# Tridiagonal reduction on one core: the next column as K times a packed vector less a part formed behind the inner product

## The reference

```python
deg = jnp.sum(A, axis=0) + jnp.sum(A, axis=1) - jnp.diagonal(A)
d_inv_sqrt = jnp.where(deg > 0, jax.lax.rsqrt(deg), 0.0)
L_norm = d_inv_sqrt[:, None] * (jnp.diag(deg) - A) * d_inv_sqrt[None, :]
_, U = jnp.linalg.eigh(L_norm)          # A is 128x128
agg = jnp.einsum('mn,bnd->bmd', U.T, features)
h = jax.nn.relu(agg @ W1 + b1)
out = jnp.einsum('nm,bmd->bnd', U, h @ W2 + b2)
```

## Time and profile before

| what | value |
|---|---|
| median of three runs | 1530.33 us (1529.59 to 1530.63) |
| profiled execution, its own time | 1528.6 us |
| its span | 1526.9 us |
| VectorE busy | 1127.4 us, 74% of the span |
| TensorE busy | 1196.6 us, 78% |
| ScalarE busy | 796.6 us, 52% |
| GpSimd busy | 511.0 us, 33% |

### The profile page before, as it was taken

The page is one execution under the profiler, slowest core; times in us unless marked ns, Lnnn a source line. Parts: engine busy times, 40 slices in busy tenths (PEclk is TensorE's granted clock), DMA queues, the critical chain, the costliest instruction groups (busy, mean ns, idle before and its releaser), DMA issues.

```text
span 1526.9 us, 26214 instructions
## 1 busy us (share of the span) xinstructions
PE 1196.6 (78%) x7121; PEld 1070.4 (70%) x7121; DVE 1127.4 (74%) x6077; ACT 796.6 (52%) x2572; POOL 511.0 (33%) x1426
## 2 busy tenths in 40 slices
PE   5666777777616600069999999999999999999998
PEld 4555666666515500058889899898998989989897
DVE  8999999999999999977757655555465555645545
ACT  1222222222319900002478687786877868778676
POOL 0288888888888888830000200000000000000000
PEclk9999999999959955569999999999999999999999
DMA  9300000000000000003100000000000000000001
GB/s 268 77 1 0 1 1 1 1 1 1 1 0 2 1 0 1 0 14 97 56 1 1 28 0 14 14 0 28 0 14 14 0 27 0 14 13 0 28 1 29
DMA packets 43625, 28.76 MB, mean 19 GB/s; under 512 B 1520, under 2 KB 39440, under 8 KB 43536
## 3 DMA queue, kind: packets, MB, share of 16 engines
q1 hardware_dynamic: 43536, 27.81, 6.7%
HBM read 19.42 MB, written 8.39 MB: 18 GB/s over the span
## 4 chain that ended last, share of the span: by engine, by line
PE 57%; DVE 38%; issue 3%; ACT 2%; ACTq 0%; DVEq 0%
PE bank L794 13%; PE bank L784 10%; PE bank L789 8%; PE bank L797 7%; PE bank L601 6%; DVE PV L1192 5%; DVE RC L1186 4%; DVE PV L1122 2%; DVE wB L935 2%; PE bank L714 2%; PE bank L766 2%; PE bank L758 2%; PE bank L722 2%; DVE sc L945 2%; PE bank L729 2%
## 5 line engine op out<-in xcount | busy, mean ns | idle before, releaser
L794 PE MATMUL bank<-spare,wT 128*128 128x256 f32 (+2 forms) x1408 | 311.2, 321 | 0.0
L530 ACT ACTIVATE PV<-bank,bias 128x256 f32<-128x256 f32 (+2 forms) x704 | 304.9, 436 | 0.0
L530 ACT ACTIVATE BIG<-bank,bias 128x128 f32<-128x128 f32 (+2 forms) x544 | 228.2, 419 | 120.2 <-PE bank L797 101.2
L794 PEld LDWEIGHTS bank<-spare,wT 128*128 128x128 f32 x1408 | 234.8, 191 | 13.2
L784 PE MATMUL bank<-spare,wT 128*128 128x128 f32 (+2 forms) x1088 | 228.1, 320 | 4.1 <-DVE spare L1429 2.7
L1415 DVE TENSOR_TENSOR BIG<-BIG,PV 128x128 f32<-128x128 f32 (+2 forms) x192 | 63.0, 328 | 206.0 <-ACT BIG L530 205.9
L784 PEld LDWEIGHTS bank<-spare,wT 128*128 128x128 f32 x1088 | 168.7, 190 | 22.5 <-DVE spare L1429 9.1
L797 PE MATMUL bank<-spare,wT 128*128 128x128 f32 (+2 forms) x768 | 169.7, 303 | 0.0
L424 ACT ACTIVATE sc<-bank 128x1 f32<-128x1 f32 x127 | 21.7, 171 | 262.3 <-PE bank L596 262.3
L596 PE MATMUL bank<-ident 128*128 128x2 f32 x254 | 74.4, 363 | 92.8 <-DVE ident L951 91.6
L789 PE MATMUL bank<-spare,wT 128*128 128x128 f32 (+2 forms) x768 | 141.6, 307 | 3.7 <-DVE spare L1427 1.2
(11 more groups left out here) (393 smaller groups left out, 2756.7 us busy)
## 6 DMA issues: line engine op xcount, KB each, us to landing
spare<-in_x SPq DMA_DIRECT2D x32, 256.0 KB, 4.1
out<-X SPq DMA_DIRECT2D x32, 256.0 KB, 2.4
spare<-in_L_gnn_Wih SPq DMA_DIRECT2D x4, 256.0 KB, 5.1
spare<-in_L_gnn_Whh SPq DMA_DIRECT2D x4, 256.0 KB, 5.0
W<-in_L_gnn_W SPq DMA_DIRECT2D x2, 64.0 KB, 2.5
Wg<-in_L_gnn_Wg SPq DMA_DIRECT2D x2, 64.0 KB, 2.2
adj<-in_adj SPq DMA_DIRECT2D x1, 64.0 KB, 1.8
X<-in_x SPq DMA_DIRECT2D x4, 0.5 KB, 17.1
```

Source lines behind the costliest of these rows:

```text
L530: last = nc.scalar.activation(gate_out[q][i][:, 0:T], gate(i, q, T), ACT.Tanh if q == GATE_G else ACT.Sigmoid, bias=bias[:, at:at + 1])
L794: last = nc.tensor.matmul(gate(i, q, T), wT[:, 0, p - 1, q * D:(q + 1) * D], xt, start=True, stop=(j == 0))
```

## The change

Three columns are no longer scaled as one triple. `UC` column 0 now holds the mask itself (not its negative). Two packed pairs are formed: (`HUM`, `HU`) = (x below the pivot, u) times h, and (`HV`, `HG`) = (mask, x below the pivot) times u_t times h, the latter as a tensor_scalar whose two scalars are both read from memory, one value per partition. Behind the inner product stand `PT` = (Au)_t HUM - ACOL, `R` = p HV + PT, `NHP` as before, and x = HG K - R. `V1`, `Z` and `T2` are gone. The wait for ScalarE's row copy moves from the inner product to the first pair. The column `ACOL` is now made by ScalarE, as an activation Copy with the mask as its scale, between L425 and L428, behind a wait for the update of `A`; VectorE waits for it ahead of the inner product. ScalarE's wait for `e_ready` goes, and the small operands count on the semaphore of the weights.

```diff
--- before.py
+++ after.py
@@ -125,7 +125,6 @@
         x_in = [sem(f"x_in{c}") for c in range(X_CHUNKS)]
         tables = sem("tables")
         weights_in = sem("weights_in")
-        small_in = sem("small_in")
         w_turned = sem("w_turned")
         w_kept = sem("w_kept")
         small_turned = sem("small_turned")
@@ -171,6 +170,7 @@
         u_ready = sem("u_ready")
         p_ready = sem("p_ready")
         a_ready = sem("a_ready")
+        acol_ready = sem("acol_ready")
         leaf_ready = sem("leaf_ready")
         leaf_sign = sem("leaf_sign")
         to_pe = sem("to_pe")
@@ -188,8 +188,8 @@
         block = ctx.enter_context(nc.Block())
 
         STEPS = N - 1
-        ST, DEN, SGE1, SGE, K3, NHP, V1, T2, Z, ACOL = range(10, 20)
-        HB, HUM, HU = range(20, 23)
+        ST, DEN, SGE1, SGE, K3, NHP, PT, R, ACOL = range(10, 19)
+        HUM, HU, HV, HG = range(20, 24)
 
         def two_sigma(k):
             return sc[:, 24 + k % 2:25 + k % 2]
@@ -273,12 +276,12 @@
...
-                sp.dma_start(t[:], t_in[name]).then_inc(small_in, 16)
+                sp.dma_start(t[:], t_in[name]).then_inc(weights_in, 16)
...
@@ -418,11 +421,11 @@
             nc.scalar.activation(m[5][:], m[4][:], ACT.Sqrt).then_inc(rs_out, 1)
             for k in range(STEPS):
                 t = k + 1
-                if k >= 2:
-                    act.wait_ge(e_ready, k - 1)
                 act.wait_ge(s_ready, k + 1)
                 nc.scalar.activation(two_sigma(k), banks[7][:, 1:2], ACT.Sqrt, scale=4.0).then_inc(sigma_ready, 1)
                 nc.scalar.activation(half_x(k), banks[7][:, 0:1], ACT.Abs, scale=0.5).then_inc(sigma_ready, 1)
+                act.wait_ge(a_ready, k + 1)
+                nc.scalar.activation(S_(ACOL), A[:, t:t + 1], ACT.Copy, scale=below[:, t:t + 1]).then_inc(acol_ready, 1)
                 if t + 1 < N:
                     act.wait_ge(xb_ready, k + 1)
                     nc.scalar.activation(uB[:, k % 2, t + 1:N], banks[0][:, t + 1:N], ACT.Copy).then_inc(row_ready, 1)
@@ -633,7 +636,7 @@
             nc.tensor.matmul(B[4], QU, QV, start=True, stop=False)
             nc.tensor.matmul(B[4], ident[:, 0:N], ident[:, 0:N], start=False, stop=True).then_inc(q_pe, 1)
 
-            pe.wait_ge(weights_in, 16 * 2 * SKIPS)
+            pe.wait_ge(weights_in, 16 * (2 * SKIPS + 10))
             for c in range(2 * SKIPS):
                 if c >= 2:
                     pe.wait_ge(w_kept, c - 1)
@@ -641,7 +644,6 @@
                     last = nc.tensor.transpose(banks[c % 2][:, q * D:(q + 1) * D], w_nat[:, c // SKIPS, c % SKIPS, q, :],
                                                ident[:, 0:N])
                 last.then_inc(w_turned, 1)
-            pe.wait_ge(small_in, 16 * 10)
             pe.wait_ge(w_kept, 2 * SKIPS)
             nc.tensor.transpose(banks[0][:, 0:N], adj[:], ident[:, 0:N])
             K = 4 * SKIPS
@@ -880,7 +882,7 @@
             V.tensor_copy(sc[:, 40:41], sc[:, 1:2]).then_inc(x_ready, 1)
 
 
-            op(V.tensor_scalar(UC[:, 0:N - 1, 0], below[:, 1:N], -1.0, None, ALU.mult))
+            op(V.tensor_copy(UC[:, 0:N - 1, 0], below[:, 1:N]))
             h = Tally(hv)
 
             def step(ins):
@@ -908,8 +910,6 @@
 
                 if k >= BN_LAG:
                     x_statistics(k - BN_LAG)
-                dve.wait_ge(a_ready, k + 1)
-                step(V.tensor_tensor(S(ACOL), A[:, nxt], below[:, nxt], ALU.mult))
                 dve.wait_ge(sigma_ready, 2 * k + 1)
                 dve.wait_ge(hv, before)
                 V.scalar_tensor_tensor(out=u_c, in0=S(SGE), scalar=sigma2, in1=x_c,
@@ -919,44 +919,42 @@
                 n_st = step(V.tensor_scalar(S(ST), s, TINY, None, ALU.add))
                 V.tensor_scalar(sg, x_t, 0.0, 0.5, ALU.is_ge, ALU.subtract).then_inc(sg_ready, 1)
                 dve.wait_ge(hv, n_st)
-                n_neg = step(V.scalar_tensor_tensor(out=S(DEN), in0=half_x(k), scalar=sigma2, in1=S(ST),
+                n_den = step(V.scalar_tensor_tensor(out=S(DEN), in0=half_x(k), scalar=sigma2, in1=S(ST),
                                                     op0=ALU.mult, op1=ALU.add))
                 dve.wait_ge(sg_ready, k + 1)
                 n_ut = step(V.scalar_tensor_tensor(out=u_t, in0=sg, scalar=sigma2, in1=x_t, op0=ALU.mult, op1=ALU.add))
-                dve.wait_ge(hv, n_neg)
+                dve.wait_ge(hv, n_den)
                 n_h = step(V.reciprocal(h_k, S(DEN)))
                 dve.wait_ge(hv, n_h)
                 dve.wait_ge(u_ready, k + 1)
-                n_nh = step(V.tensor_tensor(S(HB, 3), UC[:, k, :], h_k.to_broadcast([N, 3]), ALU.mult))
-
-                dve.wait_ge(pb_ready, k + 1)
                 if t + 1 < N:
                     dve.wait_ge(row_ready, k + 1)
-                n_k = step(V.tensor_tensor_reduce(out=wB[:, live(k)], in0=banks[1][:, live(k)], in1=uk[:, live(k)],
-                                                  scale=h_k, scalar=0.0, op0=ALU.mult, op1=ALU.add,
-                                                  accum_out=S(K3)))
-                dve.wait_ge(hv, n_nh)
-                n_v = step(V.tensor_tensor(S(V1), S(HB), u_t, ALU.mult))
-                dve.wait_ge(hv, n_k)
-                n_z = step(V.scalar_tensor_tensor(out=S(Z), in0=u_t, scalar=S(K3), in1=B[1][:, nxt],
-                                                  op0=ALU.mult, op1=ALU.subtract))
+                n_hu = step(V.tensor_tensor(S(HUM, 2), UC[:, k, 1:3], h_k.to_broadcast([N, 2]), ALU.mult))
+                n_hv = step(V.tensor_scalar(S(HV, 2), UC[:, k, 0:2], u_t, h_k, ALU.mult, ALU.mult))
+
+                dve.wait_ge(pb_ready, k + 1)
+                dve.wait_ge(acol_ready, k + 1)
+                step(V.tensor_tensor_reduce(out=wB[:, live(k)], in0=banks[1][:, live(k)], in1=uk[:, live(k)],
+                                            scale=h_k, scalar=0.0, op0=ALU.mult, op1=ALU.add, accum_out=S(K3)))
+                dve.wait_ge(hv, n_hu)
+                n_pt = step(V.scalar_tensor_tensor(out=S(PT), in0=B[1][:, nxt], scalar=S(HUM), in1=S(ACOL),
+                                                   op0=ALU.mult, op1=ALU.subtract))
+                dve.wait_ge(hv, n_pt)
                 dve.wait_ge(p_ready, k + 1)
-                dve.wait_ge(hv, n_v)
-                n_t2 = step(V.scalar_tensor_tensor(out=S(T2), in0=banks[2][:, 0:1], scalar=S(V1), in1=S(ACOL),
-                                                   op0=ALU.mult, op1=ALU.add))
+                n_r = step(V.scalar_tensor_tensor(out=S(R), in0=banks[2][:, 0:1], scalar=S(HV), in1=S(PT),
+                                                  op0=ALU.mult, op1=ALU.add))
                 n_nhp = step(V.scalar_tensor_tensor(out=S(NHP), in0=banks[2][:, 0:1], scalar=-1.0, in1=h_k,
-                                            op0=ALU.mult, op1=ALU.mult))
-                dve.wait_ge(hv, n_t2)
-
-                V.scalar_tensor_tensor(out=x_c, in0=S(HUM), scalar=S(Z), in1=S(T2),
-                                       op0=ALU.mult, op1=ALU.add).then_inc(x_ready, 1)
+                                                    op0=ALU.mult, op1=ALU.mult))
+                dve.wait_ge(hv, n_r)
+                V.scalar_tensor_tensor(out=x_c, in0=S(HG), scalar=S(K3), in1=S(R),
+                                       op0=ALU.mult, op1=ALU.subtract).then_inc(x_ready, 1)
                 dve.wait_ge(hv, n_nhp)
-                step(V.scalar_tensor_tensor(out=A[:, live(k)], in0=uk[:, live(k)], scalar=S(NHP), in1=A[:, live(k)],
+                n_a = step(V.scalar_tensor_tensor(out=A[:, live(k)], in0=uk[:, live(k)], scalar=S(NHP), in1=A[:, live(k)],
                                                   op0=ALU.mult, op1=ALU.add))
                 n_wb = step(V.scalar_tensor_tensor(out=wB[:, live(k)], in0=uk[:, live(k)], scalar=S(K3),
                                                    in1=banks[1][:, live(k)], op0=ALU.mult, op1=ALU.subtract))
                 n_sge1 = prepare_sign(k + 1) if k + 1 < STEPS else None
-                dve.wait_ge(hv, n_wb)
+                dve.wait_ge(hv, max(n_a, n_wb))
                 V.scalar_tensor_tensor(out=A[:, live(k)], in0=wB[:, live(k)], scalar=S(HU), in1=A[:, live(k)],
                                        op0=ALU.mult, op1=ALU.add).then_inc(a_ready, 1)
                 return prepare_row(k + 1, n_sge1) if k + 1 < STEPS else None
```

More of the change, by code:

```diff
@@ L204, in live, with S_ @@
             return slice(k + 1, N)
+        def S_(i):
+            return sc[:, i:i + 1]
         d16, e16 = leaf[:, 0:16], leaf[:, 16:32]
@@ L275, in _ @@
             for t, name in ((W1, "L0_gnn_W1"), (W2, "L0_gnn_W2"), (Wg0, "L1_gnn_Wg0"), (Wg1, "L1_gnn_Wg1")):
-                sp.dma_start(t[:], t_in[name]).then_inc(small_in, 16)
+                sp.dma_start(t[:], t_in[name]).then_inc(weights_in, 16)
             for t, name in ((b2B, "L0_gnn_b2"), (bg0B, "L1_gnn_bg0"), (bg1B, "L1_gnn_bg1")):
```

(6 more changed lines are left out.)

## The result

The changed kernel takes 1526.91 us (median, 1525.73 to 1527.49) against 1530.12 us for the kernel before on the same chips: ratio 0.9979, 95% interval 0.9971 to 0.9986. It is 3.2 us faster, clear of zero by the interval; 2.4 us slower, within what can be told from no change, was forecast. Its profiled execution took 1526.4 us with a span of 1524.7 us.

A forecast was written before the change was run, and what follows sets the result against it. One dependent loop through three engines, 127 steps of 2.99 us, was taken to bound the kernel. Pairs +6.1 less ACOL off VectorE 3.7 gave +2.4 us: 1532.7 against the median 1530.33, range 1527.5 to 1537.5.

The forecast's parts named there:

- ACOL on ScalarE: ScalarE's column copy, covered by TensorE's product, the dropped `e_ready` wait and the joined load semaphore: zero for all.
- Two pairs: Ahead of the inner product: first to second place needs 0.26 us, has 0.12 to 0.27; 6.1 us lost.
- ACOL off VectorE: Ahead of u (L915): the copy's slot leaves VectorE's queue; 3.7 us gained, bounds 2.6 to 7.6.
- The 1.1 us of the early steps: In 16 early steps L915 waits only for L974, 0.19 us behind it instead of 0.26; 1.1 us gained.
- Behind the inner product: Accumulator's read to new column: 0.50 us against 0.51; nothing gained or lost, bounds plus or minus 2.5 us.
- The rivals: Alternatives to the first case (chance 0.60): cheaper two-scalar slot, operation count, engine held to its end, PT held by the read.
- not 0.14 or 0.06: Second pair's two-scalar slot costs no more than one scalar, or nothing: 1528.7 or 1526.6 us; chance 0.15.
- the engine isn't held to its end: Rival: the inner product can't start before the two-scalar operation ends, place needs 0.35; 1542.7 us, chance 0.15.
- `PT` starts at the same stamp as the accumulator's read: Rival behind the inner product: PT is held by the accumulator's read, 0.08 a step, 10.2 us; 1542.9, chance 0.05.
- one VectorE operation fewer is a gain: Rival: operation count decides, 7 one-column operations between root and new x instead of 8; 7.6 us, 1522.7, chance 0.05.
- What the profile after would show: Signs: u 0.19 behind the mask's operation early; inner product 0.26 behind the first pair; late steps 0.09 to 0.14 longer.

The follow-up runs named there:

- r2: Changed kernel with ScalarE's wait for `e_ready` put back ahead of the wait for `s_ready`: 1531.39 us, ratio 1.0011 to the kernel before.
- r6: Kernel before with only the two pairs and PT, R in place of the triple and V1, Z, T2: ratio 1.0026 to the kernel before.
- r5: Changed kernel with the column copy ACOL back on VectorE, ahead of u: ratio 1.0009 to the kernel before.
- r4: Changed kernel with the two waits ahead of u (L915) swapped, VectorE's own counter first, the root second: ratio 1.0007 to the kernel before.
- r12: Changed kernel with the first pair's waits reordered: u_ready, VectorE's own counter, then row_ready: ratio 1.0022 to the kernel before.
- r11: Changed kernel with TensorE's two waits ahead of the product swapped, update of A first, u second: ratio 1.0002 to the kernel before.
- r3: Changed kernel with the wait for `e_ready` put back, but behind the wait for `s_ready`: 1527.06 us, ratio 0.9982 to the kernel before.

## Why the prediction was wrong

The step that failed is in "ACOL on ScalarE": the dropped wait for `e_ready` "asked for something two steps old", so its removal was priced at zero. That the condition had long been true was right. That the wait was therefore free was not: written first, it pushed the wait for `s_ready` into an instruction of its own, 0.06 us a step. With that wait put back in its place (r2) the kernel after loses all its gain; its removal is worth 4.9 us by time (4.4 in the loop). Added to the forecast's +2.4, it gives -2.5, near the -3.2 measured.

Added up along one path of ratios, with 1530 us as the whole (each ratio's interval is about 1.5 us to either side, so a difference of two has about 2): pairs alone +4.0 us (r6), then `ACOL` to ScalarE and the joined load semaphore -2.3 (to r2; no run has the semaphore alone), then the wait for `e_ready` away -4.9 (to the kernel after), -3.2 together.

- **Two pairs**: mechanism right, +6.1 forecast, +4.0 measured (+4.8 in the loop) for the whole of r6. The place needs 0.27 to 0.29, near the forecast 0.26. Ahead of the inner product the loss was forecast too small, not too large: +7.8 us, with 3.9 instead of 3.7 up to width 32 and 3.4 instead of 2.4 at widths 33 to 86. The slot of the two-scalar operation, put at 0.20 from two durations in the earlier trace rows, measured 0.19.
- **ACOL off VectorE**: -3.7 forecast, -2.3 measured with the wait for `e_ready` in place (-2.8 in the loop), -4.2 in the loop without it (r5 to after). A part counts for more once the other is gone, since u starts at the later of the two: the queue and the root. The 1.1 us of the early steps didn't come, since L915's second written wait took the slot over; with the other order they did (r4: 46.7 us instead of 47.8).
- **Behind the inner product**: zero forecast, -2.5 us in r6 and -2.4 in the kernel after, at the end of the stated bounds. At width 32 it is 0.50 us against 0.51, but 40 of 127 steps of the kernel before lie above 0.51 and only 4 of the kernel after. Why those steps are longer stays open. The two errors, ahead of the inner product and behind it, offset each other, so it is in part luck that the sum for the pairs came so near.
- **The rivals**: the two-scalar slot is 0.19, not 0.14 or 0.06; the inner product starts 0.19 behind an operation of 0.28, so the engine isn't held to its end; `PT` starts at the same stamp as the accumulator's read. None of them made the kernel faster. By the rule of the Trainium skill that the prediction names ("VectorE: DVE Perf Modes", section "Rules for kernel authors"), one VectorE operation fewer is a gain. That operation is `ACOL`'s, and from r6 to r2 it gains 1.4 us above width 80, 1.3 between 79 and 50 and 0.1 below 50: where the queue decides when u starts, and not elsewhere. Against the same rule's advice to count operations and not semaphores, the place of one wait cost as much as this operation.
- **What the profile after would show**: L915 starts 0.25 us behind the mask's operation in early steps, not 0.19, and 0.33 behind the root's start at width 92, not 0.25, because the root itself comes 0.06 earlier; at width 32 it is 0.21. TensorE's product ends 0.16 to 0.18 us before the inner product at widths 32 and 4, not 0.1. Steps of these widths are longer by 0.04 to 0.05 us, not 0.09 to 0.14; in r2, with the wait in place, the steps below 50 take 4.7 us more than in the kernel before.
- **What would have shown it**: the distance from new column to root in step 1 of the kernel before (0.89) beside the others (0.96), and the wait that stands there as an instruction of its own, close ahead of the root (L424, last start 389.4):

```profile
L423 ACTq EVENT_SEMAPHORE  x125: 17/17/17, 18.7 to 389.3; - x125
```

The failure was one of method: the timelines at four widths were read for what each operation costs, and a satisfied wait was taken for free.

## What to carry to other kernels

In a loop of short dependent steps, write the semaphore that arrives last first, ahead of those that are long satisfied, and drop the ones that something else implies: here one misplaced wait cost as much as an operation (4.4 and 4.2 us of the loop). Compare the first iterations, whose waits differ, with the later ones; a constant difference in the distance between two engines can be the price of a wait. And a VectorE operation on one or two columns takes a slot that grows with its scalars from memory: 0.06 to 0.08 us with none, 0.14 with one, 0.19 with two. So the count of operations doesn't tell what they cost: r6 has as many a step as the kernel before, and its loop is 4.8 us longer.

## What was not expected of the hardware

The order of written waits. With the last to arrive not written first, the instruction starts later by 0.06 us on ScalarE (root: 0.96 against 0.90) and on VectorE (L915 in r4: 0.27 against 0.21; L932 in r12: 0.25 against 0.19), and by 0.09 us on TensorE (r11: 0.36 against 0.27). The traces show the form that this takes. Of the waits ahead of one instruction the first written rides on it, and the others stand ahead of it as EVENT_SEMAPHORE instructions of the engine's queue (ScalarE: L426 in r2 and r3; VectorE: L914 in r4, L931 in r12, where one such instruction holds both other waits; TensorE: L603 in r11). When the last semaphore to arrive is one of those, that instruction ends only then, and the waiting one starts another 0.03 to 0.05 us behind its end. What the engine does in this time no run shows. The Trainium skill, "Perfetto Trace Analysis", section "Identifying Dependency Chains", says that an instruction which waits on several engines may have separate wait instructions put ahead of it; these traces agree, with 125 of them at L426 in r2.
